# A state-space layer whose two directions alternate by group of states, with one exponential for both directions' decays

## The reference, cut to what matters

```python
def _mamba(h, ...):                       # D_INNER = 512, D_STATE = 32
    x, z = jnp.split(h @ in_proj_W, 2, axis=-1)
    x = _silu(conv(x) + conv_b)           # 4 taps along time
    xdbl = x @ x_proj_W                   # -> dt, B (32), C (32)
    dt = jax.nn.softplus(xdbl[..., :DT_RANK] @ dt_proj_W + dt_proj_b)
    A = -jnp.exp(A_log)                   # 512 x 32
    def step(hst, inp):
        dt_t, B_t, C_t, x_t = inp
        dA = jnp.exp(dt_t[:, :, None] * A)
        hst = hst * dA + dt_t[:, :, None] * B_t[:, None, :] * x_t[:, :, None]
        y = jnp.einsum('bdn,bn->bd', hst, C_t)
        return (hst, y)
    ...
    return (y + Dp * x) * _silu(z) @ out_proj_W
h = ln(x) * (1 + s1) + sh1
fwd = _mamba(h); bwd = flip(_mamba(flip(h)))
x = x + g1 * (fwd + bwd)
h = ln(x) * (1 + s2) + sh2
x = x + g2 * (_silu(h @ w1) * (h @ w2) @ w3)
```

## Time and profile before

| what | value |
| --- | --- |
| median of 3 runs | 5823.47 us (5820.20 to 5830.22) |
| the profiled execution | 5820.22 us, span of the trace 5818.4 us |
| busy share | PE 95%, DVE 75%, ACT 70%, POOL 49% |
| scans, first and last start | 3109.7 and 5780.1 us |
| first scan of each batch | 3109.66, 3445.60, 3787.07, 4128.60, 4468.79, 4810.29, 5150.43, 5493.06 |
| granted TensorE clock, 3350 to 4550 us | 0.99 to 1.00 of full speed |
| statistics for the next batch between two scans (4 and 4 small operations) | 1.38 and 0.38 us |

### The profile page before, as it was taken

One profiled execution on the slowest core, in us unless ns is written; L12 is line 12 of the kernel. 1 busy time (PEld: TensorE's weight loads), 2 busy tenths in 40 slices (PEclk: granted clock), 3 DMA queues, 4 the chain that ended last, 5 costly groups with the idle time before them and its releaser, 6 DMA issues. The chain is left out here.

```text
span 5818.4 us, 74898 instructions
## 1 busy us (share of the span) xinstructions
...
## 2 busy tenths in 40 slices
...
DMA packets 175713, 228.65 MB, mean 39 GB/s; under 512 B 43121, under 2 KB 109514, under 8 KB 175090
## 3 DMA queue, kind: packets, MB, share of 16 engines
...
## 5 line engine op out<-in xcount | busy, mean ns | idle before, releaser
L2556 DVE TENSOR_TENSOR_SCAN l__h<-l__decay,psum 128x1024 f32<-128x1024 f32 x1024 | 2252.3, 2267 | 60.9 <-POOL l__hc L2522 20.6
L1960 ACT ACTIVATE l__decay<-l__dt_rep,l__a_neg 128x511 f32<-128x511 f32 x2048 | 1344.7, 709 | 50.4 <-DVE l__h L2556 46.8
L1970 PEld LDWEIGHTS psum<-ident,l__dtx_B 128*128 128x128 f32 x8192 | 884.3, 141 | 961.9 <-DVE l__h L2556 650.8
L1970 PE MATMUL psum<-ident,l__dtx_B 128*128 128x128 f32 x8192 | 1118.8, 280 | 123.5 <-DVE l__h L2556 84.5
L2522 POOL TENSOR_TENSOR l__hc<-l__h,l__c_rep 128x1024 f32<-128x1024 f32 x576 | 1145.1, 2010 | 27.0 <-DVE l__h L2556 13.2
L1936 ACT ACTIVATE l__dtx_B<-l__dtx_T,l__b_T 128x512 f32<-128x512 f32 x1616 | 1073.7, 710 | 21.1 <-PE psum L1970 15.0
L2522 POOL TENSOR_TENSOR x_sb<-l__h,l__c_rep 128x1024 f32<-128x1024 f32 x440 | 876.1, 2010 | 50.5 <-DVE l__h L2556 40.1
L684 DVE TENSOR_REDUCE l__row_max<-psum 128x1 f32<-128x512 f32 x1024 | 648.6, 680 | 207.6 <-PE psum L718 204.0
L1373 POOL TENSOR_SCALAR l__probs<-l__probs,l__rec 128x512 f32<-128x512 f32 x512 | 348.6, 694 | 886.3 <-DVE l__rec L1369 886.3
L200 POOL TENSOR_SCALAR l__ln_var_eps<-l__ln_mean_var 128x4 f32<-128x4 f32 x56 | 16.1, 287 | 1428.5 <-DVE l__ln_mean_var L186 1428.5
L2645 PE MATMUL psum<-l__hc,l__gather 128*64 128x512 f32 x2304 | 618.3, 618 | 12.0 <-POOL l__hc L2522 12.0
...
## 6 DMA issues: line engine op xcount, KB each, us to landing
l__c_rep<-l__c_dram SPq DMA_DIRECT2D x512, 128.0 KB, 2.8
l__dt_rep<-l__dt SPq DMA_DIRECT2D x256, 128.0 KB, 2.4
...
```

What stands on the lines that cost most here:

```text
L1960: nc.scalar.activation(decay[:, i % DECAYS, s, 1:T], dt_rep[:, w, c, s, 1:T], ACT.Exp, scale=a_neg[:, g, c, s:s + 1]).then_inc(S["decay"], 1)
L1970: last = nc.tensor.transpose(bx_psum(i)[:, s, t * P:(t + 1) * P], dtx_B[:, (k + 1) % 2, t, 2 * c + s, :, :].rearrange("p j d -> p (j d)"), ...
L2556: nc.vector.tensor_tensor_scan(both(h[:, i % HS, :, :]), both(decay[:, i % DECAYS, :, :]), both(bx_psum(i)), 0.0, ALU.mult, ALU.add).then_ ...
```

## The change

`split` now lets the directions alternate: block 0 is forward group 0, block 1 backward group 0, block 2 forward group 1, and so on. Eight units, both directions of one group of states, are called a cycle.

The decays get slots of their own, one for each direction and chunk (`fwd_slots`, `back_slots`), laid over memory that is free at that time: the old `decay` room, three x slots that the MLP of the previous batch has used, and a part of the weights `xproj` and `dtw`. Forward chunks 0 and 3 share a slot. In cycles 0 and 1 (units 0 to 15) ScalarE still computes single decays, with four slots; from cycle 2 on (`PAIRED`) one ACTIVATE (`decay_pair`) computes one half s of one chunk for both directions, 128x2x511. `DECAYS_AT` and `SCALES_AT` place the eight exponentials and fourteen scalings of a cycle in ScalarE's order, by the step r of the cycle, -3 to 4.

Since the weights are overwritten, SP saves them once to DRAM and loads them back at each batch's end, behind scan 123; `project_x` on TensorE waits for that. GpSimd's memsets of column 0 are split in three, and GpSimd and ScalarE wait for `dtxT_back` ahead of block 0's scalings. `pool_ops(k)` is 1 for all blocks from 2 on, where it was 1 and 2 in turn: the eighth scaling stays on GpSimd, the seventh is ScalarE's.

The order on ScalarE at the entry of a batch, before: the decays of units 3, 4 and 5 with the scalings of block 2 (body1_43 is the scan semaphore, body1_42 that of the fills, l3__dt_rep3 that of forward chunk 3).

```diff
...
-    DECAYS, HS, HCS, CS = 3, 3, 7, 4
+    HS, HCS, CS = 3, 7, 4
...
+    CYCLE = 2 * IC
+    PAIRED = 2
+    SINGLE = PAIRED * CYCLE
+    DECAYS_AT = {-3: ((0, 0), (0, 1)), -2: ((1, 0),), -1: ((1, 1), (2, 0)), 0: ((2, 1),), 1: ((3, 0),), 2: ((3, 1),)}
+    SCALES_AT = {0: (0, 1), 1: (2, 3), 2: (4, 5, 6), 3: (0, 1, 2), 4: (3, 4, 5, 6)}
...
-    pool_ops = lambda k: {0: 2, 1: 4}.get(k, 1 + k % 2)
+    pool_ops = lambda k: {0: 2, 1: 4}.get(k, 1)
...
-    DECAYED = DECAYS - 1
+    DECAYED = 2
+    decayed = lambda i: 2 * (i + 1) if i < SINGLE else 2 * SINGLE + 2 * IC * (i // CYCLE - PAIRED) + 2 * (i % IC + 1)
+    ZEROED, ZEROED_LATE = 2, 1
...
     def split(i):
-        w, g, c = i // (GROUPS * IC), i // IC % GROUPS, i % IC
-        return w, g, c
+        return i // IC % 2, i // (2 * IC), i % IC
...
-        decay = sb("decay", [P, DECAYS, 2, T], FP32)
+        room = sb("room", [P, (END - X_BASE) // 4], FP32)
+        at = lambda address: (address - X_BASE) // 4
+        SLOT = 2 * T
+        W_AT = at(89728)
+        x_at = lambda n: (KEPT + n) * SLOT
+        fwd_slots = (x_at(4), x_at(3), W_AT, x_at(4))
+        back_slots = tuple(at(147136) + n * SLOT for n in range(IC - 1)) + (x_at(5),)
+        single_slots = back_slots[0:IC - 1] + (W_AT,)
+        starts = lambda first, n: room[:, first:first + n * SLOT].rearrange("p (n t) -> p n t", t=T)[:, :, 0:1]
+        xpw_dram = nc.dram_tensor(f"{tag}_xpw_dram", (P, IC, DTL + ROWS), FP32, kind="Internal").ap()
+        dtw_dram = nc.dram_tensor(f"{tag}_dtw_dram", (ROWS, DI), FP32, kind="Internal").ap()
+        s_saved, s_back_in = nc.alloc_semaphore(f"{tag}_saved"), nc.alloc_semaphore(f"{tag}_back_in")
+
+        def slot_of(i):
+            w, g, c = split(i)
+            return single_slots[c] if i < SINGLE else (fwd_slots, back_slots)[w][c]
+
+        def decay_of(i):
+            return room[:, slot_of(i):slot_of(i) + SLOT]
+
+        def pair_of(c, s):
+            low, high = sorted((fwd_slots[c], back_slots[c]))
+            both = bass.AP(room[:, :].tensor, low + s * T + 1, [[(END - X_BASE) // 4, P], [high - low, 2], [1, T - 1]])
+            return both, low == fwd_slots[c]
...
+            scale_ops(k, (2 * c, 2 * c + 1))
+
+        def scale_ops(k, ops):
...
-            for op in (2 * c, 2 * c + 1):
+            for op in ops:
...
-                nc.scalar.activation(decay[:, i % DECAYS, s, 1:T], dt_rep[:, w, c, s, 1:T], ACT.Exp,
+                nc.scalar.activation(decay_of(i)[:, s * T + 1:(s + 1) * T], dt_rep[:, w, c, s, 1:T], ACT.Exp,
...
+
+        def decay_pair(g, c, s):
+            both, forward_first = pair_of(c, s)
+            steps = dt_rep[:, :, c, s, 1:T] if forward_first else dt_rep[:, ::-1, c, s, 1:T]
+            nc.scalar.activation(both, steps, ACT.Exp, scale=a_neg[:, g, c, s:s + 1]).then_inc(S["decay"], 1)
...
-                nc.gpsimd.memset(decay[:, :, :, 0:1], 0.0).then_inc(S["zero"], 1)
+                nc.gpsimd.memset(starts(back_slots[0], IC - 1), 0.0).then_inc(S["zero"], 1)
...
+                pool.wait_ge(*S.at("dtxT_back", IC))
...
+                if not end:
+                    pool.wait_ge(s_saved, 32)
+                nc.gpsimd.memset(starts(W_AT, 1), 0.0).then_inc(S["zero"], 1)
...
+            act.wait_ge(*S.at("dtxT_back", IC))
...
+                if end and c == 0:
+                    pe.wait_ge(s_back_in, 32 * (S.batch + 1))
...
+            sp.wait_ge(*S.at("load", 16 * LOADS))
+            sp.dma_start(xpw_dram, xpw[:, :, :]).then_inc(s_saved, 16)
+            sp.dma_start(dtw_dram, dtw[:, :]).then_inc(s_saved, 16)
...
             if begin:
+                sp.wait_ge(*S.at("scan", UNITS - IC - 1))
+                sp.dma_start(xpw[:, :, :], xpw_dram).then_inc(s_back_in, 16)
+                sp.dma_start(dtw[:, :], dtw_dram).then_inc(s_back_in, 16)
...
+                if i == ADD_AT[-1] + 1:
+                    if S.batch:
+                        pool.wait_ge(*S.at("down_filled", 0))
+                    nc.gpsimd.memset(starts(x_at(3), 3), 0.0).then_inc(S["zero"], 1)
...
+                if i == SINGLE:
+                    dve.wait_ge(*S.at("zero", ZEROED_LATE))
...
-                    dve.wait_ge(*S.at("decay", 2 * (i + 1 - DECAYED)))
+                    dve.wait_ge(*S.at("decay", decayed(i) - 2 * DECAYED))
...
-                nc.vector.tensor_tensor_scan(both(h[:, i % HS, :, :]), both(decay[:, i % DECAYS, :, :]),
+                nc.vector.tensor_tensor_scan(both(h[:, i % HS, :, :]), decay_of(i),
...
             def decays(i):
-                if i >= DECAYS:
-                    act.wait_ge(*S.at("scan", i - DECAYS + 1))
+                if i >= IC:
+                    act.wait_ge(*S.at("scan", i - IC + 1))
...
-                if i == UNITS // 2:
+                if i == IC:
...
+
+            def pairs(g, r):
+                for c, s in DECAYS_AT.get(r, ()):
+                    if g == PAIRED and c == 0:
+                        act.wait_ge(*S.at("zero", ZEROED_LATE))
+                    late = c == IC - 1 or g == PAIRED and c == IC - 2
+                    act.wait_ge(*S.at("scan", CYCLE * g + c - (2 if late else IC - 1)))
+                    decay_pair(g, c, s)
+
+            def scales_by_cycle(g, r):
+                k = 2 * g + 1 if r < 3 else 2 * g + 2
+                if r in SCALES_AT and 2 * PAIRED <= k < UNITS // IC:
+                    if SCALES_AT[r][0] == 0:
+                        act.wait_ge(*S.at("bx_filled", IC * (k - 1) - FILLED))
+                    scale_ops(k, SCALES_AT[r])
...
-                if i + DECAYED < UNITS:
+                if i + DECAYED < SINGLE:
...
-                if i + PAIRS_AHEAD < UNITS:
+                if i + PAIRS_AHEAD < SINGLE:
...
+                g, r = (i + 3) // CYCLE, (i + 3) % CYCLE - 3
+                if PAIRED <= g < GROUPS:
+                    pairs(g, r)
+                scales_by_cycle(g, r)
...
+                    act.wait_ge(*S.at("scan", UNITS - CYCLE + 1))
...
```

More of the change, by code:

```diff
@@ L74, in at @@
         return self.of[name], self.batch * self.each.get(name, 0) - lacking + n
-BASE, END = 51744, 229344
+X_BASE, BASE, END = 16512, 51744, 229344
 class Arena:
@@ L2809 @@
     (147136, 159424, "decay"),
+    (X_BASE, END, "room"),
     (147136, 159424, "x_padded"),
```

4 lines of the change are left out of this document (2 added, 2 removed).

## The result

The changed kernel takes 5832.67 us (median of 20 runs, 5826.84 to 5842.33) against 5824.24 us (20 runs, 5816.68 to 5831.61): ratio 1.0015, 95% interval 1.0009 to 1.0022. It is 8.4 us slower; the forecast (5821 against 5823.47) was 2.5 us faster. That is under the 0.2% named as indistinguishable, but with 20 runs on each side the interval excludes no change. The time lies in the forecast's range; the sign and three sizes were off.

The account below looks back on a forecast made before the run. VectorE's scans were taken to set the pace; -24 + 19 + 4.6 = -0.4, rounded to -1 on 5820.22, gave 5819, 5822 with the median's offset, and 5821 was forecast. The 8-in-10 range was 5801 to 5846 us.

Parts of the forecast that it names:

- the change-over: At unit 16 ScalarE idles until scan 15 ends; scan 20 stalls 1.15 us in four batches, 4.6 us lost.
- the entry: At unit 4 ScalarE waits for backward step sizes, delaying the tanh and scan 5: 19 us lost in all.
- the steady part: Paired exponentials and one GpSimd scaling fewer leave VectorE alone pacing: 3.0 us a batch, 24 us gained.
- case A: Rival: the wide exponential costs more than its columns say, 5841 at 1.13 us, up to 5918; chance 0.18.
- The 0.06 us per cycle: Stall before each cycle's first backward unit, from ScalarE's chain of 8.74 against 8.72 us; 0.8 us a batch.
- the 3.8 us a batch: Past a batch's entry, all that a perfect steady state can return, about 30 us in all.
- the 0.66 us: GpSimd, with one scaling fewer before the second residual addition, gives this back at scan 12.
- C: Rival: ScalarE falls behind before unit 16, 2.30 us a unit against 2.18; 1.4 us a batch, 5832; chance 0.15.
- the stall at scan 15 lets it catch up: Argument against ScalarE falling behind before unit 16: waiting for a C row there gives it time.
- four of eight batches lie under the stall at scan 18: At unit 16, the 1.15 us stall is hidden by an existing 1.37 us stall in four of eight batches.
- Nothing is charged elsewhere: The dtx wait, extra memset, saves and reloads, and the stretch between batches were taken as hidden, no cost.
- B: Rival: the entry costs nothing as step sizes land earlier or ScalarE catches up; 5802 us; chance 0.17.

Follow-up runs that it names:

- e2: Changed kernel with unit 15's exponential moved to the slot chunk 3's backward half uses later: 5832.83 us, ratio 1.0015 to the kernel before.
- e3: Changed kernel with forward blocks 0 and 1 first and unit 15 in another slot: 5798.58 us, ratio 0.9959 to the kernel before.
- e1: Changed kernel with forward blocks 0 and 1 first, directions alternating from block 4: 5806.46 us, ratio 0.9968 to the kernel before.
- e9: Changed kernel with one semaphore per chunk for the backward step sizes, order kept: 5808.38 us, ratio 0.9974 to the kernel before.
- e11: Changed kernel with forward blocks first, unit 15 in another slot, block 3's C rows first, first batch's late loads one block later: 5790.25 us, ratio 0.9947.

## Why the prediction was wrong

Scans 0 to 127 of the eight batches lose 12.5 us more than before, where the three terms summed to -0.4. Of these 12.9 us the change-over has 6.0, the entry 4.4 and the steady part 2.5. The recorded sum also has a slip: -0.4 was written on as -1, and 5822 as 5821. Carried through without it, the forecast would have been 5823, no change.

**The steady part was right in its mechanism, a little too large.** The paired group has a mean of 1136 ns, and four back to back end after 4.25 us: a period of (4.25 - 1.14) / 3 = 1.04 us, as taken. The Trainium skill, "ScalarE: Activation LUTs", What ACT_TABLE_LOAD costs, gave an estimate of 1.037 us by its terms for columns and operands, and the trace agrees; case A falls. The eight scans take 17.47 us. The 0.06 us per cycle were not there (0.02). Of the 3.8 us a batch called avoidable only about 3.3 lay past scan 24, and 0.6 of stall remained at scans 26 and 30: 21.5 instead of 24.

**The entry: right place, right chain, 23.4 instead of 19.** The wait ended 10.2 to 11.8 us after scan 0, mean 10.9 (10.8 taken). The first batch lost 4.2 us (3.4 taken). In five of the other seven the net loss is 2.0 us on average (2.2 taken). In the remaining two it is 5.3 and 3.8. In each of these about 1.1 us is a later landing (1.91 and 1.79 us of stall at scan 4, 0.73 on average in the five). For the other 2.0 and 0.7 the working had no term: TensorE goes to its lower clock. From scan 5 to 6 and from 6 to 7 in the batch at 4138.78, then in the batch at 3798.65 for comparison, in the columns of e2's rows:

```profile
4157.50:4159.70 2.20, 2.07 (x5) 1.71 (x6) 2.20 (x3) 2.20 (x4) 0.00 (x0) 0.50 0.04 7
4159.70:4163.70 4.00, 4.00 (x16) 3.35 (x15) 2.83 (x3) 1.94 (x4) 3.67 (x2) 0.56 0.00 0
...
3815.80:3818.00 2.20, 2.02 (x9) 1.82 (x10) 2.20 (x2) 2.20 (x4) 0.00 (x0) 1.00 0.00 0
3818.00:3820.80 2.80, 2.80 (x19) 2.28 (x18) 2.80 (x4) 2.80 (x6) 2.42 (x2) 1.00 0.00 0
```

(The stretch of scans 5 to 6 in the other one, at 4824.26, has 0.50 too.) Neither gets the 0.66 us back at scan 12. GpSimd in the batch at 4824.26, ahead of scan 8's product:

```profile
4850.98 2.00 POOL L2576 TENSOR_TENSOR x_sb<-l__h,l__c_rep 128x1024 f32<-128x1024 f32 x1 [1.60 <-PE psum L2721]
```

It waits 1.60 us for TensorE to free a buffer, and the head start of one scaling is gone. The fall does not need ScalarE's wait. In e3, where that wait is gone, it stands at the same place in four of batches 1 to 7, here from scan 4 to 5 in the batch at 4456.73, with a batch without it (at 3781.99) for comparison:

```profile
4468.10:4471.60 3.50, 3.36 (x13) 2.99 (x14) 3.47 (x5) 3.50 (x7) 2.99 (x3) 0.59 0.21 75
...
3793.40:3796.80 3.40, 3.29 (x22) 3.04 (x23) 3.37 (x4) 3.40 (x6) 3.18 (x3) 1.00 0.21 72
```

The four lose 6.42 to 6.44 us over scans 0 to 12, the other three 5.48, and the 6.42 of e1 is the same.

**The change-over is the step that failed: 4.6 forecast, 10.6 measured.** Two things in it. The first batch has 4.7 of the 10.6 (0.6 at scans 12 to 18, 4.1 at 18 to 24). I had rejected C with "the stall at scan 15 lets it catch up" and had this stall in six batches only; the first has none, ScalarE enters its unit 16 late, and behind that TensorE, idle for 3.19 us, fills the next unit at a mean clock of 0.53. By e9, which has hardly a wait at the entry, 3.4 of the 4.7 are the entry's wait carried past scan 12, and 1.4 are the change-over's own. And "four of eight batches lie under the stall at scan 18": that stall is no fixed property of a batch. It is TensorE's clock falling, in batches 1, 2, 4, 6 before and 1, 4, 6 after, in five with e2, in none with e3. A cover that comes and goes is no cover. Where the change-over shows, it costs 1.45 us (1.15 taken), 5.8 in batches 2, 3, 5 and 7.

**Nothing is charged elsewhere: right, though the profiled pair seems to say otherwise.** The first scan comes 5.4 us later after than before, but code ahead of the layer is the same up to two saved tables. In the thirteen profiles it starts between 3109.7 us (before) and 3119.3 (e11); e3, with the changed kernel's own start, has 3109.9. The first step of the difference is TensorE's clock, before and after:

```profile
35.00:40.00 5.00, 5.00 (x39) 5.00 (x38) 3.44 (x14) 0.00 (x0) 1.26 (x2) 0.81 0.65 214
80.00:90.00 10.00, 10.00 (x59) 2.73 (x57) 9.73 (x22) 7.26 (x8) 0.00 (x0) 1.00 0.38 119
```

```profile
35.00:40.00 5.00, 5.00 (x32) 5.00 (x31) 3.49 (x14) 0.00 (x0) 1.26 (x2) 0.65 0.63 213
80.00:90.00 10.00, 10.00 (x43) 3.01 (x42) 8.42 (x19) 6.26 (x7) 0.00 (x0) 0.78 0.78 248
```

Six of the thirteen are 3.0 to 3.4 us late by the 55th microsecond, the rest within 0.3, and later steps of 1 to 4 us follow, whose cause I did not look for. The -2.2 us behind the last scan are small beside that: 38.4 us there before, and either 36.1 to 36.2 or 37.7 to 37.8 in the versions with GpSimd's one scaling.

**The rivals.** B (the entry free, 5802) was within reach and e9 shows by what: I wrote "a whole 16 must land" as a fact of the transfers, while it was the semaphore's. C was given one size for all batches, from 3.75 operations a unit, and is true of the first only, where the entry's wait and not that count makes ScalarE late.

Not tried: what sets the landing time of the sixteen transfers (10.2 to 11.8 us), and whether TensorE kept busy at scan 15 would keep its clock.
